# Three-pass relation products, and half-precision products that nobody reads, in a two-layer graph network kernel

## The reference

```python
w = jnp.einsum('rb,bio->rio', att, basis)          # 30 bases, 2 relations, 512x512
for r in range(2):
    gate = sigmoid(x_j @ gate_w[r, :, 0]); msgs.append(gate[:, None] * x_j @ w[r])
agg = segment_sum(where(edge_type == 0, msgs[0], msgs[1]), row)
out = agg + x @ root + bias                         # done twice: h, then out
...
# layer 1, feed forward: 8 experts, 2 of them per row
logits = layernorm(x) @ Wg + bg
w, idx = top_k(logits, 2);  w = softmax(w)
h = silu(einsum('bsh,ehf->ebsf', x, W1) + b1)
y = einsum('ebsf,efh->ebsh', h, W2) + b2
x = x + einsum('ebsh,ebs->bsh', y, comb)
```

## Time and profile before

| | |
|---|---|
| median of 3 executions | 887.9 us (885.4 to 890.91) |
| the profiled execution's own time | 887.52 us |
| its span | 885.8 us |
| TensorE's mean granted clock | 0.957 of full |
| TensorE busy | 830.7 us (94% of the span) |
| VectorE / ScalarE / GpSimd busy | 527.6 / 235.4 / 148.8 us |

### The profile page before, as it was taken

How to read it: one execution, slowest core, us unless ns; L and a number is a source line. 1 busy time by engine, 2 the same in 40 slices (tenths; PEclk the granted TensorE clock), 3 DMA queues, 4 the chain that set the end, 5 groups by cost and what they waited for, 6 DMA issues and landing times.

```text
span 885.8 us, 10938 instructions
## 1 busy us (share of the span) xinstructions
PE 830.7 (94%) x4071; PEld 657.0 (74%) x4071; DVE 527.6 (60%) x746; ACT 235.4 (27%) x450; POOL 148.8 (17%) x96
## 2 busy tenths in 40 slices
PE   2999999998999999999998998989769999999997
PEld 1998758856667777764466698868758889998886
DVE  6877999936969999982267142946562211422112
ACT  3052223115411012220044242132342331323310
POOL 2010010021010000001000502600223431244210
PEclk9999998796999999999999998999769999999999
DMA  7732789984598768731040301000053121131101
GB/s 247 221 48 40 236 244 359 302 203 65 186 248 268 232 226 274 237 122 49 1 152 13 131 1 49 1 0 1 1 173 113 62 82 48 56 133 53 42 0 58
DMA packets 64211, 110.21 MB, mean 124 GB/s; under 512 B 6815, under 2 KB 16412, under 8 KB 64172
## 3 DMA queue, kind: packets, MB, share of 16 engines
q1 hardware_dynamic: 54476, 96.71, 32.9%
q0 software_dynamic: 6912, 7.70, 5.7%
q10 hardware_dynamic: 2784, 5.27, 1.6%
HBM read 105.81 MB, written 1.28 MB: 121 GB/s over the span
## 4 chain that ended last, share of the span: by engine, by line
PE 87%; DVE 8%; ACT 2%; issue 2%; DMA 1%; POOL 0%; DVEq 0%; SPq 0%; POOLq 0%
PE bank L1258 53%; PE bank L1655 13%; PE bank L1339 6%; PE bank L1462 4%; PE bank L1445 4%; PE bank L1456 2%; PE bank L1439 2%; DVE slot L1152 1%; PE bank L1267 1%; DMA slot<-in_x 1%; DVE st L861 1%; DVE slot L856 1%; ACT slot L570 1%; PE bank L1472 1%; PE bank L1274 0%
## 5 line engine op out<-in xcount | busy, mean ns | idle before, releaser
L974 DVE SCALAR_TENSOR_TENSOR weights<-weights,att 128x2048 f32<-128x2048 f32 x116 | 263.3, 2344 | 3.3 <-DMA weights<-in_L_gnn_basis 2.7
L1258 PE MATMUL bank<-half,ew_hi 128*128 128x312 f32 (+1 forms) x576 | 127.3, 310 | 2.2 <-POOL ew_lo L539 2.2
L1239 DVE CAST hid_hi<-slot 128x626 fp32r<-128x626 f32 x32 | 17.8, 557 | 159.8 <-ACT slot L817 159.8
L1258 PE MATMUL bank<-AT,slot 125*128 125x312 f32 (+1 forms) x400 | 105.9, 426 | 1.8 <-ACT slot L682 0.9
L1258 PEld LDWEIGHTS bank<-half,ew_hi 128*128 128x128 f32 x576 | 98.4, 191 | 5.9 <-issue 3.2
L1258 PEld LDWEIGHTS bank<-AT,slot 125*128 125x128 f32 x400 | 75.5, 189 | 31.8 <-ACT slot L682 1.1
L539 POOL TENSOR_TENSOR ew_lo<-weights,ew_hi 128x1024 fp32r<-128x1024 f32 x28 | 69.0, 2486 | 134.0 <-ACT ew_hi L799 134.0
L1258 PE MATMUL bank<-weights,slot 128*125 128x512 f32 (+5 forms) x306 | 90.5, 460 | 0.3 <-ACT slot L570 0.3
L1258 PE MATMUL bank<-half,ew_lo 128*128 128x312 f32 (+1 forms) x288 | 89.0, 309 | 0.0
L570 ACT ACTIVATE slot<-bank 128x312 f32<-128x312 f32 (+6 forms) x88 | 43.5, 526 | 146.9 <-PE bank L1258 107.8
L1258 PEld LDWEIGHTS bank<-weights,slot 128*125 128x125 f32 (+2 forms) x306 | 55.0, 214 | 30.2 <-issue 26.7
(11 more groups left out here) (275 smaller groups left out, 1095.1 us busy)
## 6 DMA issues: line engine op xcount, KB each, us to landing
weights<-in_L_gnn_basis SPq DMA_DIRECT2D x60, 1024.0 KB, 5.5
weights<-in_L_ffn_W SPq DMA_DIRECT2D x32, 512.0 KB, 4.4
weights<-in_L_mix_kqv_w SPq DMA_DIRECT2D x1, 3072.0 KB, 10.3
weights<-in_w_qkvT SPq DMA_DIRECT2D x3, 1024.0 KB, 5.4
slot<-slot POOLq DMA_DIRECT2D x10, 250.0 KB, 5.2
weights<-in_L_mix_mlp_w ACTq DMA_DIRECT2D x2, 1024.0 KB, 16.4
weights<-in_L_gnn_root ACTq DMA_DIRECT2D x2, 1024.0 KB, 7.8
slot<-in_row_mlp_b POOLq DMA_DIRECT2D x1, 1250.0 KB, 34.0
```

Of the source, the lines that this page charges most:

```text
L974: ins = dve.scalar_tensor_tensor(wrel[layer][r], wmat(at), att[:, layer, r, b:b + 1], wrel[layer][r], ALU.mult, ALU.add)
L1239: dve.tensor_copy(hid_hi[:, f % 4, :], hid[:, f % 4, :]).then_inc(S("hid_high"), 1)
L1258: ins = pe.matmul(out, a, b, start=i == 0, stop=i == len(pairs) - 1)
```

## The change

1. The relation products of `o2` are made in three passes of fp32r operands. ScalarE rounds Z2 into `z2_hi` (slots 2 and 3; after the eighth and the sixteenth Z2 tile) and the two weight sums into `w2_hi`; VectorE makes the remainders `z2_lo` and `w2_lo` in place. TensorE waits for `o2_low` instead of the reads of Z2 and `w_sum`.
2. A constant `busy16` (125 x 512, half precision, all ones) is filled by GpSimd at the start. `keep_busy(out, count)` issues `count` products of 512 columns of it with `ones16`; nobody reads their result. They stand: 6 after `x3r`, 4 before each of the five `xeT` tiles, 6 before the wait for `selected`, 12 before the wait for `comb`, 30 before the wait for `elist` ahead of the loop.
3. A PSUM tile `warm` is inserted after `x3r`, so every later tile moves by one bank. `claim` waits for nothing where the tile eight before is `warm`.

```diff
-              ("xqb", 4), ("xv", 5), ..., ("x3r", 5),
-              ("xeT", 5), ("el", 1), ("en", 1), ("combT", 2), ("eb2", 5), ("eh", 3)]
+              ("warm", 1), ("xeT", 5), ("el", 1), ("en", 1), ("combT", 2), ("eb2", 5), ("eh", 3)]
...
+        z2_hi, z2_lo = (half[2], half[3]), (half[5], half[6])
+        w2_hi = [t.rearrange("p (k n) -> p k n", k=KT) for t in (ew_hi[:, 1, :], ew_lo[:, 0, :])]
+        w2_lo = [ew_hi[:, 2 + r, :].rearrange("p (k n) -> p k n", k=KT) for r in range(2)]
...
+                if name == "warm":
+                    return B(stage, n)
...
+            link(pool.memset(busy16[:, :], 1.0))
...
+                    if l == 1 and n % 8 == 7:
+                        act.wait_ge(S("act_read"), READ0["Z2"] + n + 1)
+                        act.activation(z2_hi[r][:, :, 0:N], col(Z_AT[r])[:, :, 0:N], ACT.Copy).then_inc(S("o2_high"), 1)
+            for r in range(2):
+                act.wait_ge(S("w_sum"), SUM_AT[1, NB - 1, r])
+                act.activation(w2_hi[r], wrel[1][r], ACT.Copy).then_inc(S("o2_high"), 1)
...
+            dve.wait_ge(S("w_sum"), 4 * NB)
+            for r in range(2):
+                dve.wait_ge(S("o2_high"), r + 1)
+                dve.tensor_tensor(z2_lo[r][:, :, 0:N], col(Z_AT[r])[:, :, 0:N], z2_hi[r][:, :, 0:N].bitcast(f32),
+                                  ALU.subtract).then_inc(S("o2_low"), 1)
+                dve.wait_ge(S("o2_high"), r + 3)
+                dve.tensor_tensor(w2_lo[r], wrel[1][r], w2_hi[r].bitcast(f32), ALU.subtract).then_inc(S("o2_low"), 1)
             dve.wait_ge(S("A_sum"), 1)
...
-            pe.wait_ge(S("act_read"), READ0["Z2"] + 16)
             for r in range(2):
-                pe.wait_ge(S("w_sum"), SUM_AT[1, NB - 1, r])
+                pe.wait_ge(S("o2_low"), 2 * r + 2)
                 for j in range(TT):
                     for k in range(KT):
-                        ins = pe.matmul(B("o2", j)[0:P, :], col(Z_AT[r])[:, k, P * j:P * j + P], wrel[1][r][:, k, :],
-                                        start=False, stop=r == 1 and k == KT - 1)
+                        for i, (t, wt) in enumerate(((z2_hi, w2_hi), (z2_hi, w2_lo), (z2_lo, w2_hi))):
+                            ins = pe.matmul(B("o2", j)[0:P, :], t[r][:, k, P * j:P * j + P], wt[r][:, k, :],
+                                            start=False, stop=r == 1 and k == KT - 1 and i == 2)
...
+            def keep_busy(out, count):
+                for _ in range(count):
+                    ins = pe.matmul(out[0:P, :], ones16[:, :], busy16[:, :], start=True, stop=True)
+                return ins
+
+            keep_busy(claim(pe, "warm"), 6).then_inc(S("psum_full"), 1)
...
             for j in range(TT):
+                keep_busy(B("warm"), 4)
                 tile_to_cols("xeT", j, j, row(1), "xe_row")
...
             bk = claim(pe, "en")
+            keep_busy(B("warm"), 6)
             pe.wait_ge(S("selected"), 1)
...
+            keep_busy(B("warm"), 12)
             pe.wait_ge(S("comb"), 1)
...
             for n in range(3):
                 claim(pe, "eh", n)
+            keep_busy(B("eh", 0), 30)
             pe.wait_ge(S("elist"), 2)
```

More of the change, by code:

```diff
@@ L134, in gps_two_layers @@
         rng_i = sb("rng_i", [1, 16], i32)
+        busy16 = sb("busy16", [P, H], f16)
         tri16, ones16 = sb("tri16", [P, P], f16), sb("ones16", [P, P], f16)
```

## The result

The changed kernel takes 883.2 us in the median of 9 executions (879.2 to 884.0), the kernel before 887.8 us (885.4 to 890.9): ratio 0.994, 95% interval 0.9922 to 0.9958. Measured again on one chip with the experiments, as e4, it was 881.3 us beside 888.3 us, ratio 0.9919 (0.9898 to 0.994). So the change gains 0.6 to 0.8%. The profiled execution took 883.87 us with a span of 882.1 us.

The account below looks back on a forecast made before the run. TensorE was taken as the bound at the relation products and, in the tail, at first, before it waits for others. 887.5 - 6.4 - 1.9 = 879.2 us; with the median 0.4 us higher, 879.5 us, range 876.5 to 884.5.

Parts of the forecast that it names:

- rival (a): Tail: clock falls between the logits and the thirty unread products; tail +1.9 us, 883.4 us in all; chance 0.14.
- The three passes: Relation products of `o2`: 120 fp32r instructions at 0.2325 us, 28.06 us in place of 34.50; saves 6.4 us.
- The cover: Ahead of the relation products: splits cost no wait, `w2_lo[0]` ready by 407, wanted at 413.78, 7 us to spare.
- The last norm: Tail, last row norm to logits: unread products keep the clock up; -2.45 us, between -1.9 and -2.9.
- The thirty: Ahead of the expert loop: 6.6 us at full clock; first real product 0.2 us later, first 48 products -2.1 us.
- The sum: Tail, from `x3r` through the first 48 expert products: -1.9 us in all, between -2.3 and -1.5.
- A clock of 0.50 anywhere after `x3r`: Tail: a sign that would make the forecast wrong; it expected granted clock 1.00 from 625 on.
- I shift it as a whole by 6.4 us: What follows the last `o2` tile (row norm, router, SyncE loads waiting for `o2`) comes 6.4 us earlier as a whole.
- (b): Tail: unread products run at half clock; slower by 5.4 us, 893 us, or 900; chance 0.06.
- (c): Relation products: three passes gain nothing, 0.2875 us an instruction, only the tail is left, 886 us; chance 0.03.
- (d): Relation products: TensorE waits for `o2_low`, each microsecond beyond 413.78 costs one; 883 us with VectorE held until 417; chance 0.04.
- The fill of `busy16`: Kernel start: delays GpSimd's constants by about 0.5 us, at no cost, since the first statistics wait for x.

Follow-up runs that it names:

- e4: The changed kernel once more with no edit; median 881.3 us, ratio 0.9919 to the kernel before.
- e7: Changed kernel with 8 unread products instead of 30, and 28 more between relation products and the router's first transposed tile; one execution, 880.1 us.
- e9: Changed kernel, thirty kept, with 20 unread products instead of 12 in the wait for `comb`; median 878.5 us, ratio 0.9888.
- e1: Changed kernel with every `keep_busy` call and the `warm` tile taken out, three passes kept; median 881.5 us, ratio 0.9937.
- e3: Changed kernel with 8 unread products ahead of the expert loop instead of 30; median 875.9 us, ratio 0.9874.
- e8: Changed kernel with 8 unread products instead of 30 ahead of the loop and 2 instead of 4 per last-norm tile; run once, 875.7 us.
- e10: Changed kernel with 8 instead of 30, 2 per last-norm tile, and unread products ahead of the first two norms' last three tiles; 877.4 us, ratio 0.9893.
- e11: Changed kernel with 8 unread products instead of 30 and 2 instead of 4 per last-norm tile, timed; median 876.0 us, ratio 0.9877.
- e6: Changed kernel with 8 unread products instead of 30, and 4 ahead of each of the second norm's last three tiles; median 878.6 us, ratio 0.9902.
- e5: Changed kernel with none of the thirty unread products ahead of the loop, the others kept; median 875.2 us.
- e2: Changed kernel with float32 relation products and waits of before, no splits; unread products and `warm` tile kept; 886.75 us, ratio 0.9991.

## Why the prediction was right where it was, and wrong where it was not

**The number.** Forecast 879.5 us in a range of 876.5 to 884.5; measured 883.2. The gain was 0.6% in that series and 0.8% in the second (881.3), where 0.95% was forecast. The range reaches up to 883.2 only because I had stretched it for rival (a). My remark that less than 1% can hardly be told from none was too cautious: both intervals stay below 1.

**The three passes: right, in mechanism and size.** 6.4 us forecast; 51.50 to 45.00, 6.5 us, in every kernel with passes (e7, with its 28 more, aside). Each of the 120 goes by at 0.232 us, as in the earlier trace rows. The 216 ns of the Trainium skill (TensorE: Matmul & The Clock Gate, Back-to-back issue gap) would have made it 8.4. It agrees with the unread half-precision products, 0.216 us apart in e9, and not with these fp32r ones. The cover held too: ScalarE done at 404.6, VectorE's first two by 406.7, the last by 411.6, 8 us of slack where 7 were forecast, and adjacency scaled by 417.7, before the first `o2` tile at 432.

**The last norm: right.** -2.45 forecast; lastnorm fell from 18.08 to 15.68, -2.40, with clock 1.00. Both traces without unread products (before, e1) have 18.08; none of the eleven with them lost the clock in this stage. Also the price: the fours hold back the last tile, forecast 0.45 us, measured 0.46 (15.67 against 15.21 in e3 and e8).

**The thirty: the step that failed.** The sum said: six, twelve, `combT` and `eb2` at full clock, then thirty in 6.6 us, the first product 0.2 us later than before, -1.9 for the tail. The tail gained 0.1. A fall of the clock between the logits and the thirty, rival (a), which I had given 0.14, is what happened: it fell behind the 1.84 us that the twelve leave idle and the 0.79 of the copies, and the thirty took 8.1 us (+1.5), `eb2` 1.67 (+0.3). "A clock of 0.50 anywhere after `x3r`" was my own sign of being wrong. In e9, with the idle stretch filled, both prices are gone: -1.8. Why the clock fell is open all the same: e8, e10 and e11 kept it with the stretch unfilled. The rival's time of 883.4 us beside 883.2 measured is partly luck. It put the tail at +1.9; that was -0.1, for the clock was lost only with `eb2`, at 645.6, and was back at 649.0. The rest came from elsewhere: the median of the first series lies 1.9 us above that of the second against the same kernel before.

What I had seen and not drawn the conclusion from: the thirty were longer than the wait that they fill, by 2.7 us even at full clock. It became 4.8: the first expert product stood 16.8 us behind the logits where the sum has 15.4, for the half clock, and the split weights were ready 11.9 us behind them where it has 12.7. My sum took them as a cost for the clock of the first products; e3 shows that eight do as much (first48 7.07 and 7.13 us), and the 4.8 us are simply lost. My argument against (a) was one sparse stretch that kept its clock. e9 and e4, with the same TensorE program up to there, show that this very stretch keeps it in one execution and loses it in another, so one trace in which it stays is no evidence.

**What I had moved as a whole.** "I shift it as a whole by 6.4 us" held to 0.05 us in the sum up to `x3r` in e1, but not in every execution (5.0 in after, with norm1's fall) and not stage by stage: with passes norm2 took 16.95 us in seven of nine traces in which it is unfilled, where both with float32 took 15.30, and kv 25.9 instead of 27.5. The two cancel. Why the fall sits at norm2 with passes and behind keys and values without is open. norm1's fall came in after, not in e4, which is the same kernel. mid holds falls of its own: e6 and e10 were 1.5 and 0.8 us shorter there, e9 2.4 us longer.

**Rivals (b), (c) and (d)** are out: clock 1.00 in the last norm, even with two a tile; passes at 0.232 us; no wait for `o2_low`. The fill of `busy16` (0.53 us) was covered as forecast: the first statistics still waited for x. The load of x itself came 0.35 us later in that execution:

```profile
9.65 3.07 DVE L923 BATCH_NORM_STATS2 st<-slot 125x6 f32<-125x512 f32 x5 [1.56 <-DMA slot<-in_x]
```

## What to carry to other kernels

Work that only keeps the clock up belongs in a wait and must end before it does. Plan it at half clock (0.43 us a product here, 0.216 at full): as long as it is needed to bring the clock back, it runs at that price. Eight such products ahead of the loop gave 1.5 us, thirty took 3.3 away (e3, after and e5, each with four a tile); two a tile held the clock as well as four and cost 0.5 us less. One trace of a sparse stage says whether the clock held in that execution, not that it holds: compare stages across several traces before a fall is put down to an edit.

## What the runs showed of the hardware that was not expected

Up to the first root product the TensorE program is the same in all 13 traces, and it takes 393.5 to 398.5 us. Summing (1 - granted clock) x length over the windows of 2 us up to that product gives 15.4 us in e2, e4 and e5 (which reach it at 393.5 to 394.4), 17.1 in e1, e3 and e11 (394.9 to 395.2), 18.8 in before, e6, e7 and e8 (395.8 to 396.6) and 20.5 in after, e9 and e10 (397.7 to 398.5). So nearly all of this scatter, larger than what the unread products change, goes with how much clock is lost in stages that nobody edited. Whole executions agree with it: of the 45 of the kernel before that were run beside the experiments, the fastest took 884.3 us at a mean granted clock of 0.961, the slowest 892.6 at 0.948, and the others lie between in nearly the same order.

Not all of these stages are sparse by TensorE's busy time. In the kernel before, 40 products of one column each (from 143.93) stand ahead of a fall, and TensorE is busy throughout:

```profile
150.00:152.00 2.00, 2.00 (x6) 1.60 (x5) 2.00 (x2) 1.99 (x7) 0.00 (x0) 0.50 1.04 386
```

Whether a fall in one stage makes one in a later stage more or less likely (norm2 and kv changed places, e9 without norm2's fall had more in mid, e10 without either norm's had one in kv) the runs suggest and do not prove.
